# A convolution with its own weights at every position: from full 128x128 products to four 96x32 products in column groups of the array

## The chip, the cores and the metric

One Trainium2 chip (trn2); the program runs on one of its cores. The metric is the device time of one execution in microseconds, the median of several. Traces come from one profiled execution. Everything is float32 in the part concerned.

## What is computed

Two layers on x of 32 batches x 32 channels x 56 x 56. The change is in the first:

```
x = x + L0(gn(x))     # gn: every (batch, channel) plane normalised
x = x + L1(gn(x))     # attention over the 16 nearest points, then a norm
L0: patches = 3x3 neighbourhoods, padded by 1      # (b, p, i), i = 32 channels x 9 = 288
    out[b,o,p] = sum over i of patches[b,p,i] * weight[o,p,i]  + bias[o,p]
```

So each of the 3136 positions p has a weight matrix of its own, 32 x 288, used for the 32 batches only. The weights are 32 x 3136 x 288 floats, 115.6 MB.

## The kernel before

`build` runs six parts in turn: `normalise_input` (writes the normalised and padded input to DRAM as xg: channel, row, batch, column), `convolve`, `prepare`, `split_halves`, `attend` (more than four fifths of the time) and `normalise_output`. Only `convolve` is changed.

**Tiling.** The image is cut into four quarters of 14 rows each (PER = 4, QH = 14). A step of `convolve` takes the same place in each quarter at once: four positions, one per quarter q. The stage is 14 rows x 56 places; four places (SLOTS) form a group, two groups (u = 0, 1) one turn of an inner loop of 7 turns (CHUNKS). In the text "position" is such a place, and "group" four of them: 14 groups per row, 196 in all.

**A position on PE.** `w_in` holds for 128 partitions (32 output channels of each quarter) the 288 weights of a place. Three turnings (L223, `turn`; one per kernel column k, reading every third weight) put it into PSUM as 96 x 384, 96 being channels x kernel rows. ACT copies that to `w_turned` (L259). Then three products (L242), one per k, accumulate in PSUM: stationary is `w_turned[:, s, k*128:(k+1)*128]`, 96 x 128, the 32 output channels of all four quarters; moving is `windows`, 96 x 128, the 32 batches of all four quarters, one element every 58 (WP). The result is 128 x 128, of which only the four 32 x 32 blocks on the diagonal (channels of quarter q with windows of quarter q) are wanted. DVE copies these per group, with one instruction per quarter (L273), into `conv_sb`. An fp32 product is two passes, each a weight load (PEld) and a matmul (PE); a turning is one pass.

**Order.** On PE a group is: turnings of positions 0 and 1 (AHEAD = 2), turning 2, product 0, turning 3, products 1, 2 and 3 (L226 to L244). PE waits for `w_loaded` at the start of a group, for `wt_ready` (ACT's copy) before each position's products, for `copied` (DVE) once per group. `multiplied` counts positions; ACT waits for it before it overwrites a slot of `w_turned`, DVE before it copies, SP before it overwrites `windows`.

**SP's queue.** One program, in order (L181 to L197): per row three loads of `windows` (L188, 928 KB each, double-buffered by r); per group four loads of `w_in` (L195, one per quarter, 144 KB each, double-buffered by u), each behind a wait on `turned` that says that the group two before has been turned:

```
sp.wait_ge(multiplied, row * W + W)
for k in range(K): sp.dma_start(windows[k:KC:K, r, :, :], ...)
...
sp.wait_ge(turned, before + SLOTS)
for q in range(PER): sp.dma_start(w_in[C * q:C * (q + 1), u, :, :]..., ...)
```

So the windows of a row are issued behind the weights of the last group of the row before, and the first weights of the row behind the windows.

**Loops.** Every engine runs `each_half` (L170): a hardware loop over pairs of rows, in it the two rows written out, in each a hardware loop over the 7 turns, in it the two groups written out.

Elsewhere in the trace: `attend`'s L880 multiplies 128 x 32 stationary operands into four column groups of the array in turn (`ps[q:q + C, ...]` with q = 32 * (j % 4)), moving 128 columns at unit step; L861 turns 128 x 128 blocks; L838 and L842 use row groups with 392 moving columns (L842 in bf16); L481 in `prepare` has a stationary operand `feat_sb[:, par, k::28]`. L613 is `attend`'s outer loop, with a long body.

Of the kernel before, what the change touches and what calls it, by code (L numbers as in the profile page):

```python
# [12 lines left out]
BATCH, C, H, W = 32, 32, 56, 56  # L13
N = H * W
K = 3
IN_DIM = C * K * K
NEIGHBOURS = 16
P = 128
PER = P // C
GROUPS = BATCH // PER  # L20
HP, WP = H + 2, W + 2
# [6 lines left out]
QH = H // PER  # L28
# [5 lines left out]
def gate(engine, sem, value, passed):  # L34

    engine.wait_ge(sem, value)
    engine.sem_inc(passed, 1)
# [96 lines left out]
def convolve(nc, weight, xg, conv):  # L135

    SLOTS = 4
    AHEAD = 2
    CHUNKS = W // (2 * SLOTS)  # L140
    KC = K * C
    with ExitStack() as stack:
        enter = stack.enter_context
        windows = enter(nc.sbuf_tensor("windows", [KC, 2, PER, BATCH * WP], FP32))
        w_in = enter(nc.sbuf_tensor("w_in", [P, 2, SLOTS, IN_DIM], FP32))
        w_turned = enter(nc.sbuf_tensor("w_turned", [KC, 4, K * P], FP32))
        conv_sb = enter(nc.sbuf_tensor("conv_sb", [P, BATCH, QN], FP32))
        ident = enter(nc.sbuf_tensor("ident_c", [P, P], FP32))
        w_ps = enter(nc.psum_tensor("w_ps", [P, SLOTS, 512], FP32))
        conv_ps = enter(nc.psum_tensor("conv_ps", [P, 2, SLOTS, P], FP32))  # L150
        ident_ready = enter(nc.semaphore("c_ident"))
        win0 = enter(nc.semaphore("c_win0"))
        win1 = enter(nc.semaphore("c_win1"))
        w0 = enter(nc.semaphore("c_w0"))
        w1 = enter(nc.semaphore("c_w1"))
        turned = enter(nc.semaphore("c_turned"))
        wt_ready = enter(nc.semaphore("c_wt_ready"))
        multiplied = enter(nc.semaphore("c_multiplied"))
        copied = enter(nc.semaphore("c_copied"))
        out_stored = enter(nc.semaphore("c_out"))  # L160
        passed = enter(nc.semaphore("c_passed"))
        block = enter(nc.Block())
        win_loaded, w_loaded = [win0, win1], [w0, w1]
        xg_rows = xg.rearrange("c h b w -> c h (b w)")
        weight_rows = weight.rearrange("o p i -> o (p i)")

        TURN_FREE, WT_FREE, MUL_FREE, COPY_FREE = 2 * SLOTS, SLOTS, 2 * W, 2

        def each_half(engine, body):  # L170

            with engine.Fori(0, QH // 2) as t:
                for r in range(2):
                    row = t * 2 + r
                    body(row, None, None, r, None)
                    with engine.Fori(0, CHUNKS) as j:
                        for u in range(2):
                            body(row, (row * CHUNKS + j) * (2 * SLOTS) + u * SLOTS, j, r, u)

        @block.sync  # L181
        def _(sp):
            def body(row, before, j, r, u):
                if u is None:

                    sp.wait_ge(multiplied, row * W + W)
                    for k in range(K):
                        sp.dma_start(windows[k:KC:K, r, :, :],  # L188
                                     xg_rows[:, bass.ds(row + k, PER, QH), :]).then_inc(win_loaded[r], 16)
                    return  # L190

                sp.wait_ge(turned, before + SLOTS)
                for q in range(PER):
                    at = (row * W + j * (2 * SLOTS) + (u * SLOTS + q * QN)) * IN_DIM
                    sp.dma_start(w_in[C * q:C * (q + 1), u, :, :].rearrange("o s i -> o (s i)"),  # L195
                                 weight_rows[:, bass.ds(at, SLOTS * IN_DIM)]).then_inc(w_loaded[u], 16)

            each_half(sp, body)
            for q in range(PER):

                sp.wait_ge(copied, QN // SLOTS + COPY_FREE)
                sp.dma_start(conv[:, :, q * QN:(q + 1) * QN].rearrange("b c n -> c b n"),
                             conv_sb[C * q:C * (q + 1), :, :]).then_inc(out_stored, 16)
            sp.wait_ge(out_stored, 16 * PER)

        @block.gpsimd
        def _(pool):
            nc.gpsimd.memset(ident[:], 0.0).then_inc(ident_ready, 1)
            pool.wait_ge(ident_ready, 1)
            nc.gpsimd.affine_select(out=ident[:], in_=ident[:], compare_op=ALU.not_equal, fill=1.0, base=0,  # L210
                                    pattern=[[-1, P]], channel_multiplier=1).then_inc(ident_ready, 1)

        @block.tensor
        def _(pe):
            pe.sem_inc(turned, TURN_FREE)
            pe.sem_inc(multiplied, MUL_FREE)
            pe.wait_ge(ident_ready, 2)

            def turn(before, s, u):

                pe.wait_ge(wt_ready, before + (s + 1))
                for k in range(K):
                    last = nc.tensor.transpose(w_ps[0:KC, s, k * P:(k + 1) * P], w_in[:, u, s, k::K], ident[:])  # L223
                last.then_inc(turned, 1)

            def body(row, before, j, r, u):  # L226
                if u is None:
                    gate(pe, win_loaded[r], (row - r) * (8 * K) + 16 * K, passed)
                    return
                pe.wait_ge(w_loaded[u], (row * CHUNKS + j) * (16 * PER) + 16 * PER)  # L230
                for s in range(AHEAD):
                    turn(before, s, u)

                pe.wait_ge(copied, (row * CHUNKS + j) * 2 + (u + 1))
                for s in range(SLOTS):
                    if s + AHEAD < SLOTS:
                        turn(before, s + AHEAD, u)

                    pe.wait_ge(wt_ready, before + (s + 1 + WT_FREE))
                    for k in range(K):  # L240
                        x_k = windows[:, r, :, :].rearrange("p q (b w) -> p q b w", w=WP)[:, :, :, bass.ds(j * (2 * SLOTS) + (u * SLOTS + s + k), 1)]
                        last = nc.tensor.matmul(conv_ps[:, u, s, :], w_turned[:, s, k * P:(k + 1) * P], x_k,  # L242
                                                start=k == 0, stop=k == K - 1)
                    last.then_inc(multiplied, 1)  # L244

            each_half(pe, body)

        @block.scalar
        def _(act):
            act.sem_inc(wt_ready, WT_FREE)  # L250

            def body(row, before, j, r, u):
                if u is None:
                    return
                for s in range(SLOTS):
                    act.wait_ge(turned, before + (s + 1 + TURN_FREE))

                    act.wait_ge(multiplied, before + (s - SLOTS + 1 + MUL_FREE))
                    nc.scalar.activation(w_turned[:, s, :], w_ps[0:KC, s, 0:K * P], ACT.Copy).then_inc(wt_ready, 1)  # L259

            each_half(act, body)

        @block.vector
        def _(dve):
            dve.sem_inc(copied, COPY_FREE)

            def body(row, before, j, r, u):
                if u is None:
                    return
                dve.wait_ge(multiplied, before + (SLOTS + MUL_FREE))  # L270
                for q in range(PER):
                    rows = slice(C * q, C * (q + 1))
                    last = nc.vector.tensor_copy(  # L273
                        conv_sb[rows, :, bass.ds(row * W + (j * (2 * SLOTS) + u * SLOTS), SLOTS)],
                        conv_ps[rows, u, :, C * q:C * q + BATCH].rearrange("p s b -> p b s"))
                last.then_inc(copied, 1)

            each_half(dve, body)

# [1027 lines left out]
```

## Time and profile before

| what | value |
|---|---|
| median of 3 runs | 13410.56 us (13410.54 to 13423.87) |
| the profiled execution | 13393.02 us, span 13391.3 us |
| mean granted clock of TensorE | 0.841 of full speed |
| busy over the span | PE 9840.4, loads (PEld) 6672.3, DVE 11243.7, ACT 10105.9, POOL 2949.7 us |
| L242 products | 4704 matmuls, 1130.6 us busy; their loads 941.6 us |
| L259 copies by ACT | 784, 345.2 us busy |
| L273 copies by DVE | 784, 224.9 us busy |
| DMA | 476.31 MB in the span |

How to read it. The span goes from the first to the last instruction of the profiled execution; the device time lies 1.7 us around it.
### The profile page before, as it was taken

To read this page: it belongs to the slowest core of one execution; us is meant where nothing else is said; L and a number is where in the kernel's file an instruction comes from. 1 tells how busy PE (TensorE), PEld (TensorE's weight loads), DVE (VectorE), ACT (ScalarE), POOL (GpSimd) and SP (SyncE) were. 2 spreads that over 40 slices of the span, in tenths; PEclk is the share of its full clock that TensorE was granted. 3 is DMA by queue.
4 is the path that set the end of the run, shared out by engine and by line. 5 is a ranking of instruction groups with operands and counts; after the bars stand their busy time and mean duration, and the time that the engine had idled before them with its cause. 6 is when DMAs were issued, how large, how long until landed. Compare 5 with 4: busy or idle time off the path is not lost. (4 is left out here: it accounts for less than half of the span.)

```text
span 13391.3 us, 279231 instructions
## 1 busy us (share of the span) xinstructions
PE 9840.4 (73%) x91034; PEld 6672.3 (50%) x91034; DVE 11243.7 (84%) x25509; ACT 10105.9 (75%) x11352; POOL 2949.7 (22%) x1648
## 2 busy tenths in 40 slices
PE   3999856777777777777777777777777777767765
PEld 3888733444444444444444444444444444444443
DVE  1111148999999999999999999999999999999997
ACT  1222237888888888888888888888888888878876
POOL 0000002222222222222222222222222222222221
PEclk9999877888888888888888888788888888878887
DMA  8444471000000000000000000000000000000002
GB/s 132 108 111 111 113 250 25 15 15 15 15 15 15 15 15 15 15 15 15 15 15 15 15 10 9 15 15 15 15 15 15 15 15 15 15 15 15 15 3 118
DMA packets 267279, 476.31 MB, mean 36 GB/s; under 512 B 196964, under 2 KB 197348, under 8 KB 248356
## 3 DMA queue, kind: packets, MB, share of 16 engines
q1 hardware_dynamic: 261348, 407.82, 12.8%
q0 software_dynamic: 4608, 51.38, 1.1%
q8 instruction: 765, 12.53, 0.4%
q14 instruction: 558, 4.57, 0.1%
HBM read 353.59 MB, written 105.50 MB: 34 GB/s over the span
## 5 line engine op out<-in xcount | busy, mean ns | idle before, releaser
L810 POOL TENSOR_TENSOR masked<-masked,shares_a 128x784 f32<-128x784 f32 x1600 | 2929.0, 1853 | 8309.6 <-DVE top L1082 8280.0
L861 PE MATMUL psum<-ident_a,masked 128*128 128x128 f32 (+1 forms) x20000 | 3614.2, 318 | 895.4 <-ACT turned_sb L974 803.7
L974 ACT ACTIVATE turned_sb<-psum 128x512 f32<-128x512 f32 (+1 forms) x5600 | 3047.4, 555 | 1444.8 <-PE psum L861 1427.0
L861 PEld LDWEIGHTS psum<-ident_a,masked 128*128 128x128 f32 (+1 forms) x20000 | 2520.5, 160 | 2510.8 <-issue 2423.4
L1043 DVE MAX8 found<-scores 128x8 f32<-128x224 f32 x11200 | 3434.7, 376 | 125.5 <-ACT scores L953 89.0
L1082 DVE CUSTOM_DVE_ANT_0 masked<-masked,scores 128x3136 f32<-128x3136 f32 x800 | 2740.2, 3425 | 27.4
L880 PE MATMUL psum<-turned_sb,rows 128*32 128x128 f32 (+1 forms) x40000 | 2073.4, 348 | 748.4 <-ACT inverse_sb L961 748.4
L953 ACT ACTIVATE scores<-psum 128x1568 f32<-128x1568 f32 x1600 | 2355.2, 1472 | 175.4 <-DVE top L1082 144.3
L965 ACT ACTIVATE masked<-masked,minus_top 128x3136 f32<-128x3136 f32 x800 | 2348.7, 2936 | 0.0
L945 ACT ACTIVATE masked<-shares_a,own 128x3136 f32<-128x3136 f32 x800 | 2322.5, 2903 | 1.0
L880 PEld LDWEIGHTS psum<-turned_sb,rows 128*32 128x32 f32 (+1 forms) x40000 | 1597.6, 140 | 1123.1 <-issue 1122.9
L838 PE MATMUL psum<-points 32*128 32x392 f32 x12800 | 1755.2, 622 | 45.4 <-ACT scores L953 27.1
L1074 DVE SCALAR_TENSOR_TENSOR scores<-scores,bound,shares_a 128x1568 f32<-128x1568 f32 x800 | 1473.6, 1842 | 0.0
L273 DVE COPY conv_sb<-conv_ps 32x128 f32 x784 | 224.9, 287 | 1264.8 <-PE conv_ps L242 1256.5
L259 ACT ACTIVATE w_turned<-w_ps 96x384 f32<-96x384 f32 x784 | 345.2, 485 | 1122.8 <-PE w_ps L223 1122.6
L242 PE MATMUL conv_ps<-windows,w_turned 96*128 x4704 | 1130.6, 404 | 7.6
L849 PE MATMUL psum<-ones,above 128*1 128x1 f32 x1600 | 150.7, 163 | 1308.7 <-DVE rest L1123 1307.3
L242 PEld LDWEIGHTS conv_ps<-windows,w_turned 96*128 96x128 f32 x4704 | 941.6, 211 | 101.9 <-issue 24.3
L849 PEld LDWEIGHTS psum<-ones,above 128*1 128x1 f32 x1600 | 89.9, 80 | 1479.5 <-issue 1479.5
L1073 DVE TENSOR_SCALAR scores<-scores,bound 128x1568 f32<-128x1568 f32 x800 | 813.0, 1016 | 3.7 <-DVE bound L1064 2.5
L838 PEld LDWEIGHTS psum<-points 32*128 32x128 f32 x12800 | 559.2, 204 | 366.3 <-issue 366.1
L842 PE MATMUL psum<-halves_a,minus 3*128 3x392 bf16 x6400 | 636.9, 375 | 0.0
(135 smaller groups left out, 6057.1 us busy)
## 6 DMA issues: line engine op xcount, KB each, us to landing
w_in<-in_L_conv_weight_dram SPq DMA_DIRECT2D x784, 144.0 KB, 2.7
points<-unit SPq DMA_DIRECT2D x128, 392.0 KB
shares_a<-share SPq DMA_DIRECT2D x32, 1568.0 KB
windows<-xg SPq DMA_DIRECT2D x42, 928.0 KB, 10.2
xg<-padded SPq DMA_DIRECT2D x32, 406.0 KB, 15.9
table<-table_sb SPq DMA_DIRECT2D x32, 404.2 KB
rows<-table SPq DMA_DIRECT2D x32, 396.0 KB
x_in<-in_x_dram POOLq DMA_DIRECT2D x8, 1568.0 KB, 12.1
```

Source lines behind the costliest of these rows:

```text
L242: last = nc.tensor.matmul(conv_ps[:, u, s, :], w_turned[:, s, k * P:(k + 1) * P], x_k, start=k == 0, stop=k == K - 1)
L810: nc.gpsimd.tensor_tensor(m, m, shares[:, t.half, k * width:(k + 1) * width], ALU.add).then_inc(logits_ready, 1)
L838: nc.tensor.matmul(ps[:, r * BANK:r * BANK + SCH], points[C * r:C * (r + 1), t.half, t.queries()], points[C * r:C * (r + 1), t.half, at:at ...
L861: last = nc.tensor.transpose(ps[0:width, bank + u * P:bank + (u + 1) * P], masked[:, t.ring, j * P:j * P + width], ident[:])
L880: last = nc.tensor.matmul(ps[q:q + C, SUM_BANK:SUM_BANK + P], rows[0:width, t.half, j, 0:C], turned_sb[0:width, t.par, j, :], start=j < PE ...
L945: nc.scalar.activation(masked[:, t.ring, :], shares[:, t.half, :], ACT.Relu, bias=own[:, t.half, at:at + 1], scale=STEEP / SLOPE).then_inc ...
L953: nc.scalar.activation(scores[:, t.par, quad * QUAD:(quad + 1) * QUAD].rearrange("p (a b) -> p a b", b=SCH), ps[:, 0:PER * BANK].rearrange ...
L965: nc.scalar.activation(masked[:, t.ring, :], masked[:, t.ring, :], ACT.Exp, bias=minus_top[:, t.ring:t.ring + 1], accum_out=total[:, t.rin ...
L974: nc.scalar.activation(turned_sb[0:high, t.par, g * GROUP:g * GROUP + width // P, :].rearrange("p a b -> p (a b)"), ps[0:high, bank:bank + ...
L1043: n = step(nc.vector.max(found[:, t.par, c, :], scores[:, t.par, c * PART:(c + 1) * PART]))
L1074: return step(nc.vector.scalar_tensor_tensor(high, high, bound[:, 0:1], shares[:, t.half, POOL_COLS:N], ALU.subtract, ALU.min))
L1082: nc.vector.tensor_tensor_reduce(m, m, scores[:, t.par, :], 1.0, NEVER, ALU.add, ALU.max, top[:, 0:1]).then_inc(masked_ready, 1)
```

## The change

PE's products are made for each quarter by itself: stationary 96 x 32, moving 96 x 32, written to PSUM partitions 32q to 32q + 31, that is, to column group q. The order is k outside, q inside, so the four quarters take turns. Each of the four last products of a position increments `multiplied`, whose counts are multiplied by 4 everywhere. The results of all quarters lie in the same 32 columns, so DVE copies them with one instruction per group. PE's program no longer has the inner loop of 7 turns: a row is written out, and the addresses in it are constants. The other engines keep their loops; loads, turnings and ACT's copies stay.

```
-        TURN_FREE, WT_FREE, MUL_FREE, COPY_FREE = 2 * SLOTS, SLOTS, 2 * W, 2
+        TURN_FREE, WT_FREE, MUL_FREE, COPY_FREE = 2 * SLOTS, SLOTS, 2 * W * PER, 2
...
+        def each_half_written_out(engine, body):
+            with engine.Fori(0, QH // 2) as t:
+                for r in range(2):
+                    row = t * 2 + r
+                    body(row, None, None, r, None)
+                    for j in range(CHUNKS):
+                        for u in range(2):
+                            body(row, row * W + (j * (2 * SLOTS) + u * SLOTS), j, r, u)
...
-                    sp.wait_ge(multiplied, row * W + W)
+                    sp.wait_ge(multiplied, row * (W * PER) + W * PER)
...
                     for k in range(K):
-                        x_k = windows[:, r, :, :].rearrange("p q (b w) -> p q b w", w=WP)[:, :, :, bass.ds(j * (2 * SLOTS) + (u * SLOTS + s + k), 1)]
-                        last = nc.tensor.matmul(conv_ps[:, u, s, :], w_turned[:, s, k * P:(k + 1) * P], x_k,
-                                                start=k == 0, stop=k == K - 1)
-                    last.then_inc(multiplied, 1)
-            each_half(pe, body)
+                        for q in range(PER):
+                            x_k = windows[:, r, q, :].rearrange("p (b w) -> p b w", w=WP)[:, :, j * (2 * SLOTS) + (u * SLOTS + s + k)]
+                            last = nc.tensor.matmul(conv_ps[C * q:C * (q + 1), u, s, 0:BATCH],
+                                                    w_turned[:, s, k * P + C * q:k * P + C * (q + 1)], x_k,
+                                                    start=k == 0, stop=k == K - 1)
+                            if k == K - 1:
+                                last.then_inc(multiplied, 1)
+            each_half_written_out(pe, body)
...
-                    act.wait_ge(multiplied, before + (s - SLOTS + 1 + MUL_FREE))
+                    act.wait_ge(multiplied, before * PER + ((s - SLOTS + 1) * PER + MUL_FREE))
...
-                dve.wait_ge(multiplied, before + (SLOTS + MUL_FREE))
-                for q in range(PER):
-                    rows = slice(C * q, C * (q + 1))
-                    last = nc.vector.tensor_copy(
-                        conv_sb[rows, :, bass.ds(row * W + (j * (2 * SLOTS) + u * SLOTS), SLOTS)],
-                        conv_ps[rows, u, :, C * q:C * q + BATCH].rearrange("p s b -> p b s"))
-                last.then_inc(copied, 1)
+                dve.wait_ge(multiplied, before * PER + (SLOTS * PER + MUL_FREE))
+                nc.vector.tensor_copy(conv_sb[:, :, bass.ds(row * W + (j * (2 * SLOTS) + u * SLOTS), SLOTS)],
+                                      conv_ps[:, u, :, 0:BATCH].rearrange("p s b -> p b s")).then_inc(copied, 1)
```

## Rows read from the trace of the kernel before

**Rows 1.** The page's first line; then single lines' instructions: durations min/median/max ns, first and last start.
```profile
span 13391.3 us, 279231 instructions
...
L223 PE MATMUL w_ps<-ident_c,w_in x2352: 270/272/452, 199.4 to 1618.3; 128*96 128x128 f32 x196
...
L242 PE MATMUL conv_ps<-windows,w_turned x4704: 384/402/521, 201.4 to 1622.2; 96*128 x196
...
L273 DVE COPY conv_sb<-conv_ps x784: 278/286/298, 207.8 to 1623.7; 32x128 f32 x196
```

**Rows 2.** Stretches: busy us of PE, PEld, DVE, ACT, POOL; clock, DMA share, GB/s.
```profile
199.40:1622.60 1423.20, 1383.55 (x7056) 1253.38 (x7056) 223.77 (x780) 345.24 (x784) 0.00 (x0) 0.96 0.41 107
603.40:611.00 7.60, 5.06 (x24) 4.73 (x24) 1.15 (x4) 1.95 (x4) 0.00 (x0) 0.55 0.51 116
611.00:618.00 7.00, 7.00 (x38) 6.36 (x37) 1.15 (x4) 1.73 (x4) 0.00 (x0) 1.00 0.30 84
```

**Rows 3.** Waits from 190 to 1700 us: total us, times, longest.
```profile
PE w_ps L223 <- DMA w_in<-in_L_conv_weight_dram: 231.4, 14, 199.4
```

**Rows 4.** Order of time, PE: start, us to the last end, operation, count.
```profile
585.08 0.51 PE L223 MATMUL w_ps<-ident_c,w_in 128*96 128x128 f32 x3
585.42 4.19 PE L242 MATMUL conv_ps<-windows,w_turned 96*128 x18
589.44 1.16 PE L223 MATMUL w_ps<-ident_c,w_in 128*96 128x128 f32 x9
590.70 1.58 PE L242 MATMUL conv_ps<-windows,w_turned 96*128 x6
```

**Rows 5.** Order of time, PE and its loads, in attention.
```profile
5009.68 1.28 PEld L880 LDWEIGHTS psum<-turned_sb,rows 128*32 128x32 f32 x48 [1.33 <-issue]
5011.15 0.13 PEld L880 LDWEIGHTS psum<-turned_sb,rows 64*32 64x32 f32 x2 [0.20 <-issue]
...
5011.49 0.66 PE L861 MATMUL psum<-ident_a,masked 128*128 128x128 f32 x4
...
5012.07 0.31 PEld L838 LDWEIGHTS psum<-points 32*128 32x128 f32 x8 [0.17 <-issue]
5012.51 0.11 PEld L842 LDWEIGHTS psum<-halves_a,minus 3*128 3x128 bf16 x4
...
5012.84 0.35 PE L842 MATMUL psum<-halves_a,minus 3*128 3x392 bf16 x4
```

**Rows 6.** L481 in the part after the convolution: order of time, and its durations.
```profile
1734.26 4.10 PE L481 MATMUL table_ps<-to_table,feat_sb 128*112 128x132 f32 x18 [16.37 <-ACT feat_sb L438]
...
L481 PE MATMUL table_ps<-to_table,feat_sb x448: 287/364/570, 1734.3 to 1975.8; 128*112 128x132 f32 x150
```

**Rows 7.** Order of time at the start of a row, PE and ACT.
```profile
606.09 2.16 PE L223 MATMUL w_ps<-ident_c,w_in 128*96 128x128 f32 x9 [2.54 <-DMA w_in<-in_L_conv_weight_dram]
607.09 0.49 ACT L259 ACTIVATE w_turned<-w_ps 96x384 f32<-96x384 f32 x1 [6.96 <-PE w_ps L223]
607.73 0.49 ACT L259 ACTIVATE w_turned<-w_ps 96x384 f32<-96x384 f32 x1 [0.15 <-PE w_ps L223]
```

**Rows 8.** The outer loop of attention, PE's branch: min/median/max ns.
```profile
L613 PEldq COMPARE_BRANCH x15: 79/3413/3782, 2843.5 to 12643.3; - x15
```

**Rows 9.** Order of time, SP's issues before a row's end.
```profile
585.76 1.84 SPq L195 DMA_DIRECT2D w_in<-in_L_conv_weight_dram  x4
588.39 2.18 SPq L188 DMA_DIRECT2D windows<-xg  x3
```

**Rows 10.** DMA from 590 to 602 us (busy tenths, packets); loads of w_in, issue to landing.
```profile
DMA  2979997996979699695979899798997949699897
...
DMA packets 407, 2.76 MB, mean 230 GB/s; under 512 B 34, under 2 KB 34, under 8 KB 407
...
DMA to landing us min/median/max: 2.4/2.7/13.5
```

**Rows 11.** A stretch of attention, columns as in rows 2.
```profile
5100.00:7100.00 2000.00, 1488.16 (x14986) 956.53 (x14979) 1913.12 (x4365) 1724.81 (x1884) 527.23 (x288) 0.84 0.06 15
```

## The prediction, made before the changed kernel was built

> **What bounds the kernel now.** I read the page for the span, then the stage by its own lines, the table of stretches, the waits, and last the order of single instructions. The convolution runs from the first turning at 199.4 us to the last product at 1622.2 (it ends 0.4 later): 1423 us of 13391 [rows 1]. PE is busy in 1384 of them, DVE and ACT in 224 and 345, the DMA engines 41% [rows 2]. What PE waits for is a load of weights, 231.4 us in 14 waits, of which 199.4 is the start of the kernel; the other 13 stand at the row boundaries and sum to 32 us [rows 3]. So PE's own work bounds the stage, with a small DMA stall per row; the change touches nothing outside it.
>
> A group is 4 positions; the stage has 14 rows of 14 groups, (1423 - 32) / 196 = 7.1 us each. Its order on PE is 9 turnings, 6 product passes, 3 turnings, 18 passes [rows 4] (an fp32 product is two passes, each a load and a matmul). Nine turnings take 1.16 us, (1.16 - 0.27) / 8 = 0.111 each; 18 passes take 4.19, (4.19 - 0.40) / 17 = 0.223 each [rows 1, 4]. 24 x 0.223 + 12 x 0.111 = 6.7, plus slow turnings after a stall. The 24 passes are 5.35 us of a group, and they are what the change rewrites.
>
> **Why 0.223, and what a pass of 32 columns costs.** Attention's L880 already uses four column groups with loads of 32 columns and moving operands of 128: 48 loads start within 1.28 us, 0.027 apart, so a round of four takes 0.109, or 0.85 ns per moving column while four stream together [rows 5]. L242 streams as many columns in 0.223, 1.74 ns each. The differences are the step through memory (one element in 58, 232 bytes) and the 128-column load. L481 has a step on the other operand: it loads 112 columns 28 elements apart at (4.10 - 0.36) / 17 = 0.220 per pass, about 2 ns a column, with a moving operand at unit step [rows 6]. I take the step as the cause: 32 stepped columns stream in 32 x 1.74 = 56 ns, taken as 57, with the 32-column load hidden behind it, as in L880.
> The Trainium skill (Advanced Engine Details and Errata, SBUF Cachelines) says that fp32 reads which change the 16-byte line at every element pay a penalty; by that rule the new products pay it too, since their step is unchanged, and the two rows agree with it. It does not say whether four such reads at once share one penalty.
>
> So everything hangs on the time P of one round of four passes. Bounds from rows: 57 ns if the four column groups stream independently, as L880's unit-step ones do; 223 ns (4 x 56) if stepped reads take turns. Issue need not bind below L880's 27 ns per pair: L842 runs four loads in 0.11 us, each 0.10 long, and its four matmuls in 0.35 [rows 5], so pairs can start some 7 ns apart. I take P = 57, by the row that has the same column groups.
>
> **The change, part by part.**
> (1) Products. 24 passes of 0.223 become 24 rounds of P.
> (2) Changes of array shape. Turnings use 128x96, products now 96x32 in column groups. After L861's last matmul starts (5011.49 + 0.66 - 0.27, the length of one as in L223's row, = 5011.88) the next shape's load starts at 5012.07 [rows 5]: 0.20 us, of which 0.107 is the matmul's own stream, so about 0.09 is added. Today turnings and products follow without it. Four changes per group; the first turnings after one also need about 0.165 to the second matmul instead of 0.111, my reading of the same row ((0.66 - 0.27) / 3 = 0.13 mean over three intervals).
> (3) ACT. Copies of turned weights follow each other every 0.64 us (607.09, 607.73) [rows 7]. A group's first turning ends near 0.55, its copy starts at 0.66; the four run to 0.66 + 3 x 0.64 + 0.49 = 3.07. Today that is covered by 7 us; now the fourth product waits for it.
> (4) DVE. Four copies of 0.287 become one of 128 partitions; DVE is idle in five sixths of the stage, so only the last group's 0.9 us counts. Cost zero while a group is longer than 0.4.
> (5) Semaphores. 4 increments per position instead of 1; L880's last products signal too, and the load behind them waits 0.20 [rows 5], no more than a change of shape without signals. So 0; above it, at most a few hundredths of a microsecond per position.
> (6) Written out. The 5 address computations per group go; they ran under the matmuls. A body of two rows has some 6000 PE instructions instead of a small loop, so code must stream, and its 6 taken branches back should cost like attention's, median 3.4 us [rows 8]. They fall at row starts, inside the stall below: 0. If that cover is gone, 6 x 3.4 = 20 us.
>
> The group with P = 57: turnings 0 to 0.94 (last start) + 0.20, first product when its copy is in, 1.20; six rounds and the switch, 0.14 + 6P = 0.48, so turnings at 1.68, done at 2.23; second and third product from 2.16, fourth at 3.12 (copy 3.07 and 0.05); 0.14 + 6P more gives **3.60 us**. As a formula: 3.26 + 6P up to P = 0.078, 1.96 + 24P above.
>
> (7) Row boundaries. SP issues a row's windows only behind the weights of the last group, when the fourth turning of group 11 (counting from 0) is done. That was 585.59 [rows 4]; weights and windows are issued at 585.76 and 588.39 [rows 9]; while they move, DMA delivers 230 GB/s with its engines full [rows 10]; the next row's first turning starts at 606.09 [rows 7]. So 20.5 us pass from that turning to the next row's start, by SP and DMA alone, whatever PE does. Today 2.4 groups cover 17.5 of it; of 3.60 us groups 2.4 cover 8.5, and the stall per row grows from 2.5 to about 12. A row is then 11 x 3.60 + 2.23 + 20.5 = 62.3 us. In mid-row the weights are wanted 2 x 3.60 - 2.23 = 5.0 us after their release, against about 1.8 to issue and 2.7 to land [rows 9, 10]: just enough.
> (8) The clock. The stretch after a 3 us stall has a granted clock of 0.55 over 7.6 us, then 1.00 [rows 2]; its nine turnings take 2.16 instead of 1.16 [rows 7]. About one group per row is slow so, +1.2 us.
>
> **Sum.** 13 x (62.3 + 1.2) + 14 x 3.60 + 1.2 = 877 us for the stage, 546 less, and 0.9 from DVE. The profiled execution took 13393.0 (span 13391.3), so 12846; the median of the runs shown is 17.5 above that execution, which gives 12864. I say 12855, 4.1% less. A third of the stage's new time is the stall and its slow restart, so halving the group does not halve the row.
>
> **Rivals.**
> *The pace of pairs binds* (15%). No row shows load-and-matmul pairs sustained under 27 ns for long. At 109 ns a round the group is 1.96 + 24 x 0.109 = 4.58, a row 11 x 4.58 + 2.5 + 20.5 + 0.8 = 74.2, the stage 1030: 12999. For it: 27 ns is the best long run in the trace. Against: there each pass streams 128 columns, which explains it without an issue limit.
> The Trainium skill (TensorE: Matmul & The Clock Gate, Wait — 56ns, not 53.3ns?) puts a floor of about 25 ns between matmul starts however few columns; by that figure, an estimate, a round is 100 ns and the time about 12970. L880's 27 ns agrees with the rule, L842's short burst does not.
> *Stepped reads take turns* (10%), **the slower case**: P = 223. The group is 7.31, a row 80.4 + 3.2 + 20.5 + 0.5 = 104.6, the stage 1462: 13430 to 13450, slower by 0.3%. The same price holds if the four products do not run side by side at all, that is if the change does not do what it says. The point where it turns: 157 x (1.96 + 24P) + 78P + 305 = 1423 gives P = 0.21. Against it: L880's independent groups.
> *The clock stays low* (6%). The product passes use few columns and PE idles 12 us per row. With turnings at 0.213 and switches 0.15 longer, a group is 4.7 and the stage 1046: 13015. Against: attention, with PE idle a quarter of the time, is granted 0.84 [rows 11], and the levels are 1.2 and 2.4 GHz, so two thirds of it run at the upper one.
> *Code does not stream fast enough* (5%). A group has 24 + 192 loads and matmuls and about 12 others. A missed block of code costs 3.4 us [rows 8]; once per group without cover it is 7.0 us a group and only some tens of us saved, 13300 to 13400.
> My forecast, with P between free and 65, has 60%: 12790 to 12920. About 4% is left for others.
>
> **Numbers.** 0.2% is what a measurement of this kernel can tell from no change. Faster: forecast, pace, clock and most of the code case, 0.87; slower 0.09, same 0.04. The range takes in the forecast's own, the pace and the clock, 0.81: 12790 to 13040.
>
> **What would show it.** In the profile after: a stage from 199 to about 1076; groups of 3.6 us; six rounds of 24 passes within about 0.6 us; four idle gaps of PE's loads per group at changes of shape; ACT's copies at an unbroken 0.64 and PE waiting for the fourth; 13 waits for weights of about 12 us instead of 2.5; DMA share near 0.65; granted clock about 0.85. Wrong if a round is near 109 or 223, if PE idles for nothing the profile shows inside a run of products, or if the row stall is not 20.5 us less the cover.

## The result, and the profile after

The changed kernel takes **12950.2 us** (median of 4 runs, 12942.0 to 12953.1) against 13411.1 for the kernel before: a ratio of 0.9653, 95% interval 0.9636 to 0.9670, 3.5% faster. 12855 was predicted, with 12790 to 13040 as the range. The profiled execution took 12949.0 us, span 12947.2, 444 less than before [rows 1], where 547 were expected. A later set of runs (experiment 11) gives the same picture: 0.9645 (0.9629 to 0.9661).

The page after, its first lines and the three groups of the stage (L253 stands in an answer of its own below):

```profile
span 12947.2 us, 304970 instructions
...
PEclk9887788888887888888888888888888788878877
DMA  9666700000000000000000000000000000000003
...
q8 instruction: 944, 15.47, 0.5%
...
L284 DVE COPY conv_sb<-conv_ps 128x128 f32 x196 | 57.1, 291 | 953.8 <-PE conv_ps L253 953.8
L272 ACT ACTIVATE w_turned<-w_ps 96x384 f32<-96x384 f32 x784 | 343.7, 486 | 646.8 <-PE w_ps L233 644.3
...
L233 PE MATMUL w_ps<-ident_c,w_in 128*96 128x128 f32 x2352 | 375.1, 299 | 438.8 <-DMA w_in<-in_L_conv_weight_dram 437.3
```

DVE's copies went from 224 to 57 us, ACT's work is what it was, and the line to stop at is the last: the turnings now wait 437 us for weights, where they waited 231 [rows 3]; the start of the kernel is 218.5 of the one and 199.4 of the other, so what is left grew from 32 to 219. q8 is the queue that fetches program code in blocks of 16 KB: 944 of them in the span, 765 before.

The product line's instructions, and the stage as one stretch with the two behind a row boundary (columns as in rows 2):

```profile
L253 PEld LDWEIGHTS conv_ps<-windows,w_turned x18816: 106/127/160, 220.6 to 1156.9; 96*32 96x32 f32 x199
L253 PE MATMUL conv_ps<-windows,w_turned x18816: 215/238/263, 220.6 to 1157.0; 96*32 96x32 f32 x199
```
```profile
218.50:1157.00 938.50, 704.60 (x21168) 580.03 (x21168) 56.83 (x195) 343.73 (x784) 0.00 (x0) 0.89 0.64 165
563.00:567.60 4.60, 4.51 (x108) 3.62 (x108) 0.00 (x0) 1.95 (x4) 0.00 (x0) 0.57 0.02 6
567.60:572.00 4.40, 3.60 (x122) 2.87 (x112) 0.58 (x2) 1.74 (x4) 0.00 (x0) 1.00 0.65 185
```

The stage runs from 218.5 to 1157.0: 938.5 us against 1423 [rows 2]. PE is busy in 75% of it instead of 97%; DMA went from 0.41 to 0.64. A group in order of time, from the middle of a row (as rows 4, with ACT):

```profile
538.21 1.23 PE L233 MATMUL w_ps<-ident_c,w_in 128*96 128x128 f32 x9
538.91 1.24 ACT L272 ACTIVATE w_turned<-w_ps 96x384 f32<-96x384 f32 x3 [1.23 <-PE w_ps L233]
539.45 0.38 PEld L253 LDWEIGHTS conv_ps<-windows,w_turned 96*32 96x32 f32 x24 [0.23 <-ACT w_turned L272]
539.45 0.55 PE L253 MATMUL conv_ps<-windows,w_turned 96*32 96x32 f32 x24
539.93 0.57 PE L233 MATMUL w_ps<-ident_c,w_in 128*96 128x128 f32 x3
540.43 1.28 PE L253 MATMUL conv_ps<-windows,w_turned 96*32 96x32 f32 x72
```

72 matmuls start within 1.28 - 0.24 = 1.04 us, where 18 took 3.79 before: a round of four takes 0.060 us (from the first start of a run of 72 to the 69th are 17 rounds; median over the unbroken runs, read from single instructions) instead of 0.223 for one pass. The group is done 3.42 us after it began. Then the boundary of the same row, SP and PE:

```profile
543.24 2.06 SPq L198 DMA_DIRECT2D windows<-xg  x3
546.63 6.23 SPq L205 DMA_DIRECT2D w_in<-in_L_conv_weight_dram  x8
```
```profile
542.92 2.14 PE L233 MATMUL w_ps<-ident_c,w_in 128*96 128x128 f32 x9 [1.20 <-DMA w_in<-in_L_conv_weight_dram]
...
553.00 1.18 PE L253 MATMUL conv_ps<-windows,w_turned 96*32 96x32 f32 x65 [2.94 <-issue]
563.09 2.16 PE L233 MATMUL w_ps<-ident_c,w_in 128*96 128x128 f32 x9 [8.92 <-DMA w_in<-in_L_conv_weight_dram]
```

The last line is the large stall, from 554.2 to 563.1. The two others are new: PE waits 1.20 us for weights in the middle of the flow, and at 553.00 it resumes a run of products after 2.94 us in which it waited for nothing the profile shows.

**Where the 938.5 us are.** Counted from the starts of single loads: 196 groups of 3.42 = 670; 13 stalls at row boundaries, 170; 101 short waits for weights inside rows, 58; the first group of each row 1.2 longer, 17; pauses inside runs of products, 13. Sum 928; the other 10 are spread over the groups in pieces too small to name.

### The profile page after: what moved, and what is told of

Read it like the earlier page. It is cut to its first block and busy times, and to the rows that moved or that the text cites. A ratio compares the mean times of both kernels' runs of the same rounds, so it can differ in the third digit from the quotient of the medians.

```text
span 12947.2 us, 304970 instructions
## 1 busy us (share of the span) xinstructions
PE 9126.0 (70%) x105146; PEld 5952.5 (46%) x105146; DVE 11081.8 (86%) x24921; ACT 10096.9 (78%) x11352; POOL 2951.5 (23%) x1648
## 5 line engine op out<-in xcount | busy, mean ns | idle before, releaser
L889 PE MATMUL psum<-turned_sb,rows 128*32 128x128 f32 (+1 forms) x40000 | 2024.2, 342 | 769.3 <-ACT inverse_sb L970 769.3
L889 PEld LDWEIGHTS psum<-turned_sb,rows 128*32 128x32 f32 (+1 forms) x40000 | 1555.1, 137 | 1136.9 <-issue 1136.9
L847 PE MATMUL psum<-points 32*128 32x392 f32 x12800 | 1787.4, 633 | 76.2 <-issue 33.8
L284 DVE COPY conv_sb<-conv_ps 128x128 f32 x196 | 57.1, 291 | 953.8 <-PE conv_ps L253 953.8
L233 PE MATMUL w_ps<-ident_c,w_in 128*96 128x128 f32 x2352 | 375.1, 299 | 438.8 <-DMA w_in<-in_L_conv_weight_dram 437.3
L1128 DVE SCALAR_TENSOR_TENSOR bound_low<-over,best,margin 128x2 f32<-128x2 f32 x800 | 583.5, 729 | 28.5
## 6 DMA issues: line engine op xcount, KB each, us to landing
x_in<-in_x_dram POOLq DMA_DIRECT2D x8, 1568.0 KB, 13.1
```

Of the source, the lines that this page charges most:

```text
L847: nc.tensor.matmul(ps[:, r * BANK:r * BANK + SCH], points[C * r:C * (r + 1), t.half, t.queries()], points[C * r:C * (r + 1), t.half, at:at ...
L889: last = nc.tensor.matmul(ps[q:q + C, SUM_BANK:SUM_BANK + P], rows[0:width, t.half, j, 0:C], turned_sb[0:width, t.par, j, :], start=j < PE ...
```

## The experiments

Twelve runs in three sets, each set beside the kernel before on the same chip: there it took 13393, 13389 and 13395 us, so ratios or differences to these are what counts. Experiments 2 to 6 and 12 were executed once, so their times are single values; the main readings from them are of their traces.

**1. PE's row written out, products as before.** The function `each_half_written_out` of the change, and

```
-            each_half(pe, body)
+            each_half_written_out(pe, body)
```

> The kernel before with PE's row written out, its full 128x128 products kept. My theory: code has to be streamed (some 7 blocks of 16 KB per row instead of none), and a block being fetched holds up SP's issues of weight loads; with groups of 7 us the weights still land in time, so the stage stays at 1423 us and the time at 13411, within 0.2%. Some tens of SP's 784 issues of w_in last over 0.6 us instead of 0.316. Rival A: SP's long issues of the changed kernel come from DMA traffic, not from code: then none is long here. Rival B: streaming code costs PE itself: the stage is over 20 us longer.

Measured 13415.6 (10 runs) against 13393.1: 1.0017 (1.0007 to 1.0027). The stage runs from 195.8 to 1630.2, 1434 us, some 10 more than before: a group is 0.07 us shorter (15 us in all), and the gaps between rows are 21 us longer in sum, above all at every second one (5.0 to 6.2 us), where PE branches back. So writing out alone costs 0.2%; rival B is right in kind and half as large as stated; the rest of the 22 us is in attention (experiment 12). Of SP's 784 issues of w_in, 2 last over 0.6 us, so my "some tens" was wrong. But with 68 code blocks in the stage only 6 issues began within 0.5 us after the start of one, so this run says little of what such a meeting costs; experiment 3 has 28 of them.

**2. Order of the products turned round.**

```
-                    for k in range(K):
-                        for q in range(PER):
+                    for q in range(PER):
+                        for k in range(K):
```

> The changed kernel with the order of the 12 products of a position turned round: quarter outside, kernel column inside, so that six passes in a row go to the same column group. If the gain comes from four column groups streaming side by side and matmuls start in order, a position's 24 passes take about 4 x 5 x 0.057 + 0.1 = 1.2 us instead of 0.35, a group 6.7 us, and the time is near 13390, the gain gone. Rival: PE runs ahead freely into other column groups, or the gain comes only from the shorter operands: no change, 12950.

Measured 12989.3 against 13393.1. A run of 72 passes in order of time:

```profile
601.86 0.57 PE L233 MATMUL w_ps<-ident_c,w_in 128*96 128x128 f32 x3
602.36 1.75 PE L253 MATMUL conv_ps<-windows,w_turned 96*32 96x32 f32 x72
```

72 passes take 1.75 us instead of 1.28; they start 0.021 us apart on average, four of them in 0.085. Passes to one column group follow each other every 0.058 us (experiment 3), so six in a row for each group, started in program order, would make 72 passes last 3.5 us. As they take less than half of that, PE does run ahead into the next column groups, between two and three of them at once (0.058 / 0.021); my premise was false, and the order k outside, q inside is worth 0.8 us a group, not 3. As groups are then 4.2 us long, only 5 short waits for weights are left: of 196 x 0.78 = 153 us, 70 reach the time.

**3. All products in one column group.** Column groups taken away, everything else kept (written out, short operands):

```
-   matmul(conv_ps[C * q:C * (q + 1), u, s, 0:BATCH], ...)     # k outside, q inside; DVE copies once
+   matmul(conv_ps[0:C, u, s, C * q:C * (q + 1)], ...)         # q outside, k inside; DVE copies per quarter
```

> The changed kernel with all four quarters' products written to PSUM partitions 0 to 31, side by side in the free dimension, so that all passes go to one column group; DVE copies per quarter as before the change; the output is the same. A pass of 32 stepped columns streams in 0.056 us, so a position's 24 passes take 24 x 0.056 = 1.34 us and a group about 1.96 + 24 x 4 x 0.056 = 7.3 us: the gain is gone, time near 13410. Rival: a pass is over sooner (0.03 us) and issue set the pace all along: a group under 5 us, time under 13100.

Measured 13618.1 against 13395.2: not only is the gain gone, it is 1.7% slower than before.

```profile
605.75 1.23 PE L233 MATMUL w_ps<-ident_c,w_in 128*96 128x128 f32 x9
606.98 1.57 PE L253 MATMUL conv_ps<-windows,w_turned 96*32 96x32 f32 x24
608.47 0.57 PE L233 MATMUL w_ps<-ident_c,w_in 128*96 128x128 f32 x3
608.97 4.34 PE L253 MATMUL conv_ps<-windows,w_turned 96*32 96x32 f32 x72
```

72 passes in 4.34 - 0.24 = 4.10 us, 0.058 apart, here and in the median. One column group alone sustains one pass per 0.058 us, four side by side sustain four passes in 0.060. That settles what pays: the column groups, and nearly the whole factor of four. (With the stage's clock at 0.83 and groups of 7.5 to 8.7 us it comes out above the kernel before, and above my sum.) And of the 28 issues of w_in that began within 0.5 us after the start of a code block, 16 lasted over 0.6 us here, in groups more than twice as long and with the DMA engines 0.37 busy.

**4. Unit step in the kernel before.**

```
-   x_k = windows[:, r, :, :].rearrange(...)[:, :, :, bass.ds(j * (2 * SLOTS) + (u * SLOTS + s + k), 1)]
+   x_k = windows[:, r, 0, bass.ds(j * (2 * SLOTS) + (u * SLOTS + s + k), P)]
```

> The kernel before with its moving operand read at unit step (128 neighbouring elements of one quarter's windows; the values are others, the count of elements is the same). If the step of 58 elements is what makes a pass 0.223 us, a pass takes 0.109 us, a group 4.3 us, a row 11 x 4.3 + 3 + 20.5 = 71 us, and the time is near 12990. Rival: the pass is long for its 128-column load or its 96 rows: it stays at 0.22, and the time at 13411.

```profile
601.52 0.93 PE L242 MATMUL conv_ps<-windows,w_turned 96*128 x6
602.28 0.49 PE L223 MATMUL w_ps<-ident_c,w_in 128*96 128x128 f32 x3
602.62 2.17 PE L242 MATMUL conv_ps<-windows,w_turned 96*128 x18
```

(2.17 - 0.27) / 17 = 0.112 a pass against 0.223 [rows 4]. The same loads, rows and columns: the step alone doubled the pass. The stage runs from 197.1 to 1191.1, 994 us. The time is 12904.1 against 13393.1, but 50 us of that are attention's, which is shorter on these other values (11229 us from its first load to the last part, 11281 in the kernel before). The Trainium skill (Advanced Engine Details and Errata, SBUF Cachelines) names a penalty for accesses that change the 16-byte line each time, without its size; the trace agrees and gives the size: a step of 232 bytes costs 0.223 / 0.112 = 2. That holds at the upper clock. In the runs of products at a granted clock of 0.5 a pass takes 0.213 us at unit step and still 0.223 with the step, so there the step costs next to nothing.

**5 and 6. Unit step in the changed kernel, with 32 and with 64 moving columns.**

```
-   x_k = windows[:, r, q, :].rearrange("p (b w) -> p b w", w=WP)[:, :, j * (2 * SLOTS) + (u * SLOTS + s + k)]
+   x_k = windows[:, r, q, j * (2 * SLOTS) + (u * SLOTS + s + k):][:, 0:BATCH]        # or 0:2 * BATCH
```

> The changed kernel with its moving operands read at unit step (32 neighbouring elements; other values, same count). If stepped reads set the round of four passes (0.061 us in the trace after), it falls to between 0.027 and 0.045, and a run of 72 passes from 1.28 us to 0.7 to 1.0. The time hardly moves (12900 to 12950), because weights then bound the row. Rival: issue of pairs sets the round: it stays at 0.061.

> The kernel with unit step (r_unit_after), with 64 moving columns per product instead of 32; half of the result is not used. There a round of four took 0.054 us, twice the 0.027 that 32 columns stream in. If the issue of eight loads and matmuls sets 0.054, it stays at 0.054 with 64 columns (0.053 of streaming). If a load of 0.027 stands in series with each matmul, it goes to 0.080.

At the upper clock and inside a position, a round of four takes 0.033 us with 32 columns at unit step, 0.055 with 64, and 0.060 with 32 stepped ones (medians, read from single instructions; the first round of a position is longer). So the stepped read does set the round, and 0.027 to 0.045 was right. The 0.054 that the text above starts from is the length of a whole run of 72, 0.924 us, over 17, and in that run PE mostly waits. The group shows it, with 32 columns at unit step:

```profile
543.93 0.52 PEld L253 LDWEIGHTS conv_ps<-windows,w_turned 96*32 96x32 f32 x48
544.12 0.49 ACT L272 ACTIVATE w_turned<-w_ps 96x384 f32<-96x384 f32 x1 [0.34 <-PE w_ps L233]
544.65 0.28 PEld L253 LDWEIGHTS conv_ps<-windows,w_turned 96*32 96x32 f32 x24 [0.20 <-ACT w_turned L272]
```

The second and third product are through in half a microsecond; the fourth waits until ACT has copied its weights, and its first matmul starts 0.053 us after that copy ends. In the changed kernel this distance is 0.053 too, and 0.07 at most in 194 of 196 groups: there PE comes to the fourth product at about the moment at which its copy is in. ACT's copy is thus as close a limit as the products, and a faster round shortens the group from 3.43 us only to 3.12. The stage does not gain even that: 943 and 944 us, against 929 for the changed kernel (experiment 11). With 32 columns at unit step the groups give back 60 us, but the short waits for weights grow from 58 to 87 us, pauses for nothing the profile shows from 12 to 32, and the granted clock falls from 0.89 to 0.84. The times, 12876.9 and 12879.5, are lower for attention's part alone, some 50 us shorter on other values. With 64 columns the stream sets the round (64 x 0.85 = 0.054), so a load is hidden behind the matmuls. What sets the 0.033, the stream of 0.027 or the pace of starts (7 ns from one matmul to the next in a round), is not shown.

**7. One DMA per group of weights.**

```
-   for q in range(PER): sp.dma_start(w_in[C * q:C * (q + 1), u, :, :]..., weight_rows[...])
+   sp.dma_start(w_in[:, u, :, :]..., weight_quarters[:, :, bass.ds(at, SLOTS * IN_DIM)])    # "o (q n) i -> q o (n i)"
```

> The changed kernel with the weights of a group loaded by one DMA over 128 partitions instead of four over 32. The 93 waits for weights in the changed kernel (219 us without the first) are 13 of about 13.5 us at row boundaries and 80 short ones inside rows, some 50 us. My theory: the short ones come from SP's issues, of which a fetch of PE's code holds up some, on a round trip with 0.3 us to spare. One issue frees 1.5 us of it: the short waits vanish, the row stall stays, the time falls by 40 to 60 us to about 12900. Rival: the DMA engines' rate bounds the groups: no change.

Measured 13430.0 against 13388.8: 1.0029 (1.0017 to 1.0040), far off. PE waits 799 us in 196 waits for weights, 199 of it the kernel's start. While these loads run, between row boundaries, the DMA engines are 0.2 busy at about 100 GB/s:

```profile
DMA  7222222222222122222222221222212222223999
GB/s 161 108 92 104 112 105 105 94 58 88 113 103 105 53 101 103 103 112 57 84 85 101 103 95 63 95 92 105 101 54 79 89 105 105 76 82 107 233 208 232
```

0.2 of 16 engines is 3 to 4, and in 71% of the stage exactly four packets are under way at once (in the changed kernel in 1%). The Trainium skill (DMA: Bandwidth & Descriptors, Rules for kernel authors) says that a DMA whose outermost size is c, under 16, stays on at most c engines; here c is 4, and the trace agrees. The experiment says nothing of the issue time, and it is a warning: four small DMAs were faster than one large.

**8. Four buffers for weights.** `w_in` gets 4 buffers instead of 2, SP's row is written out so that the buffer is `(r * 14 + j * 2 + u) % 4`, `TURN_FREE` is 4 * SLOTS.

> The changed kernel with four buffers for weights instead of two, SP's row written out for it. The round trip has two groups (6.8 us) more. Short waits inside rows vanish: 40 to 60 us less. At the row boundary SP runs two groups further ahead, so windows are issued 6.8 us earlier and the stall falls from 13.5 to 7 us or so, unless the DMA rate binds: 13 x 6.8 = 88 us more. Together about 12810. Rival: rate-bound (2.8 MB of windows and 0.6 MB per group at 230 GB/s): a row moves 11 MB and can't be under 48 us.

Measured 12877.9 against 13388.8: 0.9618 (0.9602 to 0.9634), some 36 us better than the changed kernel, where 12810 in all was expected. After the first load PE never waits for weights:

```profile
PE w_ps L235 <- DMA w_in<-in_L_conv_weight_dram: 196.6, 1, 196.6
PE conv_ps L257 <- issue: 104.2, 64, 5.0
PE w_ps L235 <- issue: 60.1, 15, 9.1
```

What came in its place are waits for nothing the profile shows, 164 us in 79, inside runs of products and before turnings. They end in a fixed way: the 63 pauses over 0.5 us inside runs of products end 1.29 to 1.61 us (5% to 95%) after the end of a code block's transfer, while only 9% of all instants of the stage lie 1.25 to 1.7 us behind one. In the changed kernel and in experiments 2, 9, 10 and 11 it is 1.2 to 1.7 too. So PE waits for its own program. Why the blocks come late is not shown: the transfer of one takes 1.23 us in this stage and 0.98 to 1.13 in attention, so the transfer itself is little slower beside the weights and windows.

**9. Windows in pieces.** Two buffers; the windows of the next row in 12 loads, one behind the weights of each of groups 2 to 13 (SP written out, xg one row longer so that the last row's pieces have a source):

```
+   g = j * 2 + u
+   if g == 2: sp.wait_ge(multiplied, (row + 1) * (W * PER) + W * PER)
+   if g >= 2: load piece g - 2 of row + 1: windows[k:KC:K, 1 - r, q, :] <- xg_rows[:, row + 1 + k + q * QH, :]
```

> The changed kernel with the windows of the next row loaded in 12 pieces, one behind the weights of each of groups 2 to 13, two buffers for weights. If the stall at the row boundary is the transfer of windows issued in one lump behind which the weights queue, it vanishes (13 x 13.5 = 175 us); each group's DMA becomes 5 issues and 0.82 MB, 3.6 us at 230 GB/s, so groups take 3.8 to 4.5 us instead of 3.85 on average: time 12790 to 12870. Rival: the rate binds all the same and the row stays at 67 us: no change.

Measured 12820.8 against 13388.8: 0.9580 (0.9564 to 0.9596). The stage is 831 us, rows of 57 to 62 instead of 67 to 71. The boundary stalls are gone: 30 us in all are left there, nearly all at the six boundaries where PE branches back (4.1 to 4.7 us each); but there are 114 short waits inside rows, 76 us.

**10. Both.** 

> Both: windows in 12 pieces and four buffers for weights. Then only PE (3.43 us a group) and the DMA rate (11 MB a row, 48 us at 230 GB/s, 3.45 us a group) bound the row: 48 to 54 us, the stage 690 to 760, the time 12700 to 12780. Rival: SP's queue, 5 issues a group and those held up by code, binds: as with two buffers.

Measured **12807.6** against 13388.8: 0.9566 (0.9550 to 0.9582), 0.8 points below the changed kernel and 4.3% under the kernel before. Beside experiment 9 it is 13 us less, which the two intervals do not tell apart. The stage is 827 us, with 192.7 us, the kernel's start, as its only wait for weights:

```profile
PE w_ps L249 <- DMA w_in<-in_L_conv_weight_dram: 192.7, 1, 192.7
PE conv_ps L271 <- issue: 70.7, 79, 2.5
PE w_ps L249 <- issue: 35.1, 15, 4.7
```

It stops short of the 690 to 760 us expected, and not for DMA rate (share 0.74) or for weights: rows take 59 us, of which 48 are groups; the pauses for code, 106 us with the branch back, are most of the rest. The branch back, now without cover, costs 4.0 to 5.0 us at six of the 13 boundaries and 0.2 lies at the others.

**11 and 12. The changed kernel and the kernel before again.**

> The changed kernel once more, unaltered, beside the kernel before on the same chip, as the base of the other runs and to see what varies by itself. In its first trace the part ahead of the convolution took 218.5 us instead of 199.4, in six of seven experiments 194 to 199: I expect about 196 here, so that 19 us of that trace were chance. The convolution again 930 to 945 us, SP's issues of w_in over 0.6 us again near 80, attention again some 20 us longer than in a kernel with PE's loop.

> The kernel before once more: the part ahead of the convolution 194 to 200 us, the convolution 1423, and attention (first load of points to first load of y_all) 11260 to 11285 us, against 11300 to 11317 in the kernels with PE's row written out. If attention is as long here as there, its 20 us are chance and not a cost of the longer program.

The changed kernel: 12920.4 against 13395.2, 0.9645 (0.9629 to 0.9661). Its stage runs from 198.3 to 1127.2, 929 us, so the 218.5 of the first trace, 19 us more, is no part of the change. Two lines of w_in's instructions in the first trace after:

```profile
L205 SPq DMA_DIRECT2D w_in<-in_L_conv_weight_dram x784: 315/316/1802, 203.1 to 1149.7; - x196
...
  PE w_ps L233: 437.3, 93
```

The median issue lasts 0.316 as before, but 82 of 784 last over 0.6, up to 1.8, in both traces of this kernel; in both of the kernel before none does. In the first trace they begin 0.0 to 0.8 us (5% to 95%) after the start of a code block's transfer and end 1.3 to 1.8 us after it; of issues that begin 0.1 us or more before a code block, none is long. I took the waits for weights inside rows apart, group by group (101 in the first trace, 58 us). In 58 of them, 36 us, an issue was held up: 2.5 us from the first of the four issues to the last instead of 1.53, then 2.7 us to PE's start. In the other 43, 22 us, the issues were on time and the data late, 3.4 us; the 1.20 us wait above is one of these. Why those landed late was not tested. Of the 81 groups inside rows without a wait, 24 had a held-up issue too. Attention, from its first load of points to the first load of y_all, takes 11281 and 11287 us in the two traces of the kernel before, 11299 to 11317 in all nine with a written-out row and the right windows. So its 20 us are no chance, but nothing was tried that shows their cause.

## Why the prediction was right, and where it was off

*What bounds the stage, and (1), the product rounds.* Right: P was put at 57 ns and is 60, and the experiments confirm both halves: four column groups stream independently (3), and the step doubles the stream (4, and 0.033 against 0.060 in 5). The 24 passes of 5.35 us became 24 rounds of 1.44.

*(2) Changes of shape.* Right: 0.50 us lie between the start of three turnings and the next product, 0.20 of it from the last turning's start.

*(3) ACT.* The mechanism is half right: the fourth product does start when its copy is in and 0.05 later. The pace was wrong: the 0.64 us between copies was read at a row start at the lower clock [rows 7], where the turnings come 0.21 apart, three in 0.64. It was their pace, not ACT's. After, three copies take 1.24 together, so 0.38 apart, and the fourth, which follows the fourth turning and not the third copy, ends at 2.90 instead of 3.07. PE waits 0.02 us for it, not some 0.3. The group is 3.42, not 3.60: some 30 us too many in the sum.

*(4), (5).* DVE and the semaphores cost nothing on the path, as said.

*(6) Code.* Mis-sized at 0. The branches did fall under the stalls (experiment 10, without that cover, shows their price of 4 to 5 us each), but the stream of blocks costs 13 us in pauses of PE, and by holding up SP's issues some 36 us of the next term.

*(7) The row boundary.* The mechanism is right, the stall 13.1 us on average instead of 12.0, 14 us more in the sum. The step that failed is "just enough": the weights in mid-row had 0.5 us to spare on a round trip of 4.5, and the group came out shorter than expected, which left less than 0.1 (2 x 3.42 - 2.29 against 4.5). With 101 short waits 58 us stand where I had 0, five eighths of them behind issues held up by code. That is the largest term missed. Experiments 2 (a longer group) and 8 (more buffers) both remove these waits. That code fetches hold issues up rests on their timing in all runs with code blocks, not on a kernel without code blocks at this pace, which was not tried.

*(8) The clock.* Right: 0.57 in the first 4.6 us after a stall, and the first group 1.2 us longer.

*Sum.* 877 predicted for the stage, 938 and 929 measured: 877 - 30 (3) + 14 and + 58 (7) + 13 (6) gives 932. Outside it I had 0: 20 us more in attention, and 19 in the first trace ahead of the stage, whose cause is not known. That the errors of (3) and of (7) have opposite signs is luck.

*Rivals.* The pace of pairs (27 ns) did not bind: pairs of load and matmul go 15 ns apart for a whole run of 72, and 8 ns at unit step (experiment 5). The floor of about 25 ns between matmul starts that the Trainium skill gives (TensorE: Matmul & The Clock Gate, Wait — 56ns, not 53.3ns?) does not hold here; the measurement decides. Stepped reads do not take turns. The clock did not stay low (0.89). The code rival was the right place to look, at a tenth of the price I gave it; once the waits for weights are gone, its price is 106 to 164 us (experiments 10 and 8).

## What to carry to other kernels

When an engine's work in a loop is cut to less than half, redo the round trip of its loads with the new length: here two buffers with four issues of 0.5 us and a landing of 2.8 had microseconds to spare before and nothing after, and a lump of 2.8 MB in the queue stood for 13 us of stall per row. Before taking to column groups for small products, look at the step of the moving operand; in this kernel unit step alone took the stage from 1426 to 994 us (experiment 4), if the data could be laid out so. Nor do gains of the two add up: with both, the fourth product waits for ACT's copy and the row for its weights (experiment 5). And a written-out program has to be fetched: 15 KB of code per group of 3.4 us, and PE and SP's issues both paid for it.

## What the runs showed of the hardware

- Four column groups sustained four fp32 passes of 96 x 32 by 32 stepped columns in 0.060 us, at unit step in 0.033; one group alone one stepped pass in 0.058. PE also overlapped column groups when six passes in a row belonged to one of them (0.085 for four).
- A moving operand at a step of 232 bytes streamed at half the rate of one at unit step (0.223 and 0.112 us for 128 columns) at the upper clock; at the lower one both took about the same (0.223 and 0.213).
- A DMA issue by SP that started within half a microsecond after the start of a code fetch took over 0.6 us, most often 1.2, instead of 0.32 in two of three cases (54 of 83; in experiment 3, 16 of 28); of those that started 0.1 us or more before a fetch none did. With a code fetch every 21 us (experiment 1) it was 2 of 784 issues.
- PE resumed 1.3 to 1.6 us after the end of the transfer of the code block it waited for (63 pauses of experiment 8), and a branch back to code that was not there cost 4.0 to 5.0 us (experiment 10).
- One DMA over 128 partitions with an outermost size of 4 kept four packets under way at once; with four DMAs over 32 partitions each there were mostly 13 or more while data moved.
